# A two-layer graph network on one core: edge lists prepared in another order on three engines, and the first product in two float32r parts instead of plain float32

## The chip, the cores and the metric

The program runs on one core of a Trainium2 chip. The metric is the device time of one execution in microseconds; a kernel's time is the median of several executions. In the profile PE is TensorE, DVE is VectorE, ACT is ScalarE, POOL is GpSimd and SP is SyncE.

## The reference

There are 625 nodes with 512 features and 20,625 edges (10,000 drawn pairs in both directions, and a loop at each node).

```
layer 0:  xw = x @ W.T
          deg = counts of destinations (with a loop at each node), dinv = rsqrt(deg)
          h  = sum over edges of dinv[src]*dinv[dst]*xw[src], plus b
          h  = gelu(batch_norm(h)*gamma + beta) + x
          x1 = layernorm(x + h)
layer 1:  two RGCN layers with 2 relations: w[r] = sum over 30 bases of att[r,b]*basis[b]
          (30 x 512 x 512 for each layer), a gate sigmoid(x @ gate_w[r]) per edge,
          messages summed over edges, plus x @ root + bias; relu between them
          out = layernorm(x1 + that)
```

## The kernel before

The edges become two dense count matrices, one for each relation, held in `B` (sources by destinations, 5 chunks of 125 sources). `T` = 162 tiles of 128 edges in `NG` = 27 groups of six go through TensorE: for each group VectorE writes one-hot rows of the source's place in its chunk (`oh_src`) and of a key made of chunk, relation and the destination's place in a window of 16 nodes (`oh_key`), TensorE multiplies them into `psE` (two buffers), and VectorE adds two windows of each group to `B` (`add_window`). Edges are sorted by destination, so a window of 16 destinations holds three tiles; the first destination of each (`base`) is read into a register (`window_at`, one load for each window). Where a span of destinations is wider than a window, further rounds follow, under a branch on `more_i`; `rounds()` works that number out on VectorE.

All engines run programs written by hand, in order, with semaphores between them. What the change touches:

- **The front.** The three edge lists are loaded as integer rows (`edge_rows`), cast to float in one piece (`rows_f`), turned by TensorE (`edge`), copied out by VectorE, and the smallest and largest destination of each window go the same way (`mm`, `gmm`, `base`). A chain of small VectorE operations makes `place_pairs` and `key_pairs`.
- **The attention coefficients.** `att_t` is loaded on ScalarE's queue, spread by TensorE (`att`), and `build_S` makes from it the stationary operand `S` of the basis product. VectorE does this within group 0, ahead of the one-hots of group 1.
- **The basis product.** 64 loads of 1 MB go through a ring of four buffers (`basis_ring`, on SP's queue). Load n is issued when part n-4 has been used. `basis_part` multiplies a load on TensorE; four parts fill one half of `psW`; two halves are merged on ScalarE and VectorE (`w_first`, `w_merge`, `w_high`, `w_low`). The places of these parts in TensorE's order are written as numbers: `basis_upto(n)` does all parts up to n, and rounds down to whole pairs.
- **The first product.** `turn` transposes x and W in 128-blocks, `turned_out` copies them out on ScalarE, and `xw_part` does the 20 steps of x @ W.T in float32, between the groups of the loop.
- **After the loop.** VectorE sums the relations of `B` (`counts_of`, some by way of ScalarE) into `AT`; TensorE counts degrees (`deg`, 25 matmuls); POOL takes the power (`dinv_p`); ScalarE and VectorE make `z`, the scaled xw in two parts; `aggregate0(f, halves)` multiplies z by AT for the feature block f. Basis parts stand between these. After the blocks all parts up to 31 are done, and then the transposes `("g", c)` of the gelu's result. From there on nothing is changed but line numbers.

TensorE's main results go round four PSUM banks in the order of the list `uses`: a use waits until the one four places ahead of it has been released.

## Time and profile before

| | us |
|---|---|
| median of 3 runs (range) | 314.32 (312.93 to 317.32) |
| profiled execution | 314.59 |
| its span | 312.7 |
| TensorE matmuls busy | 276.0 (88%) |
| VectorE busy | 160.3 (51%) |
| ScalarE busy | 89.5 (29%) |
| mean granted clock | 0.96 |

The profiled execution is 0.3 us over the median, and 1.9 us of it lie outside the span. TensorE is the busiest engine as a mean, but a busy matmul in the profile includes its latency, and stages have limits of their own. The stages are: a front up to the first one-hot at 14.1 us; the 27 groups up to 78.4 us; degrees, z and the first aggregation up to 92.6 us; the other three feature blocks up to 118.7 us; and the rest.

### The profile page before, as it was taken

The page shows a single profiled execution, that of the slowest core. Times are in us where ns is not written, and L with a number is a line of the kernel's source. Part 1 is how long each engine was busy: PE and PEld are TensorE (multiplying, and loading weights), DVE is VectorE, ACT ScalarE, POOL GpSimd, SP SyncE. Part 2 cuts the span into 40 slices and gives each one's busy share as a digit, 9 for nine tenths or more (in the row PEclk, how much of TensorE's full clock was granted, in tenths as well). Part 3 has the DMA queues.
Part 4 walks back from the last instruction along what each step waited for, and adds up shares of the span by engine and source line. Part 5 has one row for each costly group of instructions (what it writes and reads, how often), then busy time and mean ns, then how long its engine had stood idle before and what let it go on. Part 6 is the DMA issues. An engine that isn't in the chain of part 4 may idle for free.

```text
span 312.7 us, 4598 instructions
## 1 busy us (share of the span) xinstructions
PE 276.0 (88%) x1687; PEld 180.8 (58%) x1687; DVE 160.3 (51%) x362; ACT 89.5 (29%) x140; POOL 38.3 (12%) x73
## 2 busy tenths in 40 slices
PE   1589958989799977679999999999997999999991
PEld 1573413433566643237765656677774878787770
DVE  3888888884656856855221241342434225334443
ACT  5160220201436876551352104112212242100000
POOL 2001000000292106500000000000005500011111
PEclk9999986999779999779999999999999999999997
DMA  6998992999989999958994897976002400001112
GB/s 164 231 418 326 353 410 80 415 375 369 364 259 307 413 398 426 371 183 299 388 379 171 366 343 283 419 286 265 21 1 52 118 0 0 0 2 33 33 33 66
DMA packets 12802, 73.63 MB, mean 235 GB/s; under 512 B 2000, under 2 KB 2243, under 8 KB 4588
## 3 DMA queue, kind: packets, MB, share of 16 engines
q1 hardware_dynamic: 11330, 70.82, 60.7%
q0 software_dynamic: 1104, 2.36, 2.9%
q8 instruction: 13, 0.21, 0.3%
q10 hardware_dynamic: 346, 0.17, 0.2%
q14 instruction: 9, 0.07, 0.1%
HBM read 72.05 MB, written 1.28 MB: 235 GB/s over the span
## 4 chain that ended last, share of the span: by engine, by line
PE 62%; DVE 16%; DMA 8%; issue 7%; DVEq 3%; ACT 1%; POOL 1%; ACTq 0%; POOLq 0%
PE psW L515 15%; PE psM L496 9%; PE psM L497 8%; PE psM L498 8%; PE psM L753 7%; DMA basis_ring<-in_L_gnn_basis_dram 7%; PE psM L773 6%; DVE B L1081 4%; DVEq L1071 2%; PE psM L563 2%; DVE oh_key L1088 2%; PE psE L596 2%; DVE oh_src L1088 2%; DMA rows_i<-in_edge_type_dram 1%; PE psM L639 1%
## 5 line engine op out<-in xcount | busy, mean ns | idle before, releaser
L515 PE MATMUL psW<-basis_ring,S 128*32 128x512 f32 x512 | 67.9, 646 | 6.3 <-DVEq L1057 3.7
L1267 DVE SCALAR_TENSOR_TENSOR zg<-psM,gate,zg 125x512 fp32r<-125x512 f32 x20 | 15.0, 751 | 56.9 <-ACT zg L929 56.9
L515 PEld LDWEIGHTS psW<-basis_ring,S 128*32 128x32 f32 x512 | 13.5, 114 | 41.2 <-issue 27.4
L496 PE MATMUL psM<-w,hlT 128*125 128x512 f32 x80 | 32.4, 405 | 0.1
L498 PE MATMUL psM<-w,hlT 128*125 128x512 f32 x80 | 31.7, 396 | 0.0
L497 PE MATMUL psM<-w,hlT 128*125 128x512 f32 x80 | 31.7, 396 | 0.0
L929 ACT ACTIVATE zg<-psM,gate 125x512 fp32r<-125x512 f32 x20 | 13.8, 688 | 46.3 <-PE psM L498 45.9
L596 PEld LDWEIGHTS psE<-oh_key,oh_src 128*125 128x125 f16 x162 | 13.9, 143 | 22.4 <-issue 17.3
L753 PEld LDWEIGHTS psM<-BB,zg 125*128 125x128 f32 x160 | 23.1, 188 | 3.4 <-issue 2.5
L753 PE MATMUL psM<-BB,zg 125*128 125x320 f32 (+1 forms) x160 | 24.1, 309 | 0.0
L773 PE MATMUL psM<-zg,BB 125*125 125x512 f32 x100 | 24.0, 394 | 0.0
L1081 DVE TENSOR_TENSOR B<-B,psE 125x160 f32 x54 | 17.5, 324 | 11.1 <-issue 6.6
L596 PE MATMUL psE<-oh_key,oh_src 128*125 128x160 f16 x162 | 17.0, 245 | 6.9 <-DVE B L1081 6.8
L563 PE MATMUL psM<-w0T,xT 128*125 128x512 f32 x40 | 21.7, 634 | 0.0
L773 PEld LDWEIGHTS psM<-zg,BB 125*125 125x125 f32 x100 | 18.6, 186 | 4.7
L480 POOL DMA_DIRECT2D root_raw<-in_L_gnn_root_dram x16 | 7.9, 501 | 106.8 <-DVE hlT L1297 106.8
L496 PEld LDWEIGHTS psM<-w,hlT 128*125 128x125 f32 x80 | 14.8, 185 | 9.0 <-issue 2.5
L1088 DVE TENSOR_TENSOR oh_key<-iota_f,key_pairs 128x960 f16<-128x960 f16 x27 | 17.7, 654 | 0.3
L498 PEld LDWEIGHTS psM<-w,hlT 128*125 128x125 f32 x80 | 14.8, 185 | 3.8
L497 PEld LDWEIGHTS psM<-w,hlT 128*125 128x125 f32 x80 | 14.8, 185 | 3.4
L1067 DVE TENSOR_TENSOR w<-w_both,w 128x512 fp32r<-128x512 f32 x16 | 13.1, 861 | 7.1 <-ACT w L816 6.5
L800 ACT ACTIVATE w_half<-psW,mask_h 128x512 f32<-128x512 f32 x16 | 10.1, 679 | 20.0 <-PE psW L515 20.0
(154 smaller groups left out, 381.0 us busy)
## 6 DMA issues: line engine op xcount, KB each, us to landing
basis_ring<-in_L_gnn_basis_dram SPq DMA_DIRECT2D x64, 1024.0 KB, 7.3
root_raw<-in_L_gnn_root_dram POOLq DMA_DIRECT2D x32, 64.0 KB, 3.6
xs<-in_x_dram SPq DMA_DIRECT2D x1, 1120.0 KB
out_dram<-xs SPq DMA_DIRECT2D x5, 224.0 KB
w_raw<-in_L_gnn_W_dram SPq DMA_DIRECT2D x4, 256.0 KB, 9.6
bias_b<-in_L_gnn_bias_dram POOLq DMA_DIRECT2D x1, 250.0 KB, 3.5
xs<-in_x_dram SPq DMA_DIRECT2D x1, 130.0 KB
out_dram<-xs SPq DMA_DIRECT2D x5, 26.0 KB
```

The lines of the kernel that those rows point to most:

```text
L496: nc.tensor.matmul(o, l_hi, r_hi, start=start, stop=False)
L497: nc.tensor.matmul(o, l_hi, r_lo, start=False, stop=False)
L498: last[0] = nc.tensor.matmul(o, l_lo, r_hi, start=False, stop=stop)
L515: m = nc.tensor.matmul(psW[32 * j:32 * j + 32, cc % 2, :], S[:, cc % 2, cc // CH, q].rearrange("p k r -> p (k r)"), ring[:, n % RING, j, : ...
L563: last[0] = nc.tensor.matmul(bank(("xw", c))[0:PC, :], xT[:, k, n], w0T[:, k], start=(k == 0), stop=(k == KC - 1))
L596: nc.tensor.matmul(psE[0:PC, g % 2, at:at + KEYS], oh_src[:, g % 3, j * P:j * P + PC], oh_key[:, t % OH, :], start=(j % SG == 0), stop=(j ...
L753: last[0] = nc.tensor.matmul(bank(("h", f, h))[:, 0:n], zg[:, i, d, r, f * P:(f + 1) * P], BB[:, at:at + n], start=(d + r + i == 0), stop= ...
L773: last[0] = nc.tensor.matmul(bank(("out", c))[0:PC, :], BB[:, at:at + PC], zg[:, i, d, r, :], start=False, stop=(d == NC - 1 and r + i == 2))
L929: nc.scalar.activation(zg[:, 0, c, r, :], bank(("Z", L, c, r))[0:PC, :], ACT.Copy, scale=gate[:, L, c, r:r + 1]).then_inc(zg_hi, 1)
L1081: v.tensor_tensor(to, to, psE[0:PC, g % 2, h * KEYS:(h + 1) * KEYS] .rearrange("p (c t w) -> p c t w", c=NC, t=R), ALU.add).then_inc(win_a ...
L1088: return v.tensor_tensor(out, pair.unsqueeze(1).broadcast_to(shape), pairs[:, first:first + n].unsqueeze(2).broadcast_to(shape), ALU.is_equal)
L1267: link(v.scalar_tensor_tensor(out=zg[:, 1, c, r, :], in0=bank(("Z", L, c, r))[0:PC, :], scalar=gate[:, L, c, r:r + 1], in1=zg[:, 0, c, r, ...
```

## The change

- The rows of destinations, sources and relations have semaphores of their own. VectorE casts only the destinations; ScalarE casts the other two, and copies the turned destinations out of PSUM. VectorE reads the turned sources and relations straight from PSUM. Chunk numbers come from a scaling and a rounding by a large constant, where four comparisons stood. Keys beyond a window are marked by 1024 in one combined operation.
- `B` is cleared by POOL, where ScalarE did it, and the number of further rounds is worked out by POOL, in the idle time of its front.
- `build_S` has four operations and no clearing, where it had eight and one.
- The register of `more_i` is loaded in group 14, and those of the last four windows in groups 23 to 26, between the two windows of the group, where all five stood behind the loop.
- x and W are held as an upper and a lower float32r part. TensorE turns them (`turn`), ScalarE copies the upper part out, TensorE multiplies it by the negative identity into the same bank (`take_upper`), and ScalarE copies the rest out. `xw_part` then does three float32r matmuls (`mm3`) for one in float32.
- All five chunks of x are turned before the loop, two of them and one `take_upper` ahead of the matmuls of att; W is turned in groups 2 and 3.
- In the loop the basis parts go up to 15 (17 before) and start at group 5 (3 before); parts 16 and 17 stand within the degrees, behind the second source chunk; 18 and 19 behind the transposes of vec; 20 and 21 behind the first aggregation. Block f = 1 is followed by 22 and 23 and block f = 2 by 24 to 27. The first merge moves from group 13 to 17, its lower part from 15 to 19.

```diff
-        for a in range(3):
-            use(("edge", a), "dve")
+        use("dst", "act")
         use("minmax", "dve")
+        use("src", "dve")
+        use("etype", "dve")
...
-        FIRST_IN = 23
+        FIRST_IN = 21
...
-        PARTS_IN = 17
-        FIRST_TURNS = 3
-        TURN_AT = {0: (3,), 1: (4, 5), 2: (6, 7), 3: (8,)}
-        ROUNDS_AT = 12
-        MERGE_AT = {13: 0}
-        LOW_AT = {15: 0}
+        TURN_AT = {0: (("rest", NC - 1),), 2: (("turn", NC), ("turn", NC + 1), ("rest", NC)),
+                   3: (("rest", NC + 1), ("turn", NC + 2), ("turn", NC + 3), ("rest", NC + 2)), 4: (("rest", NC + 3),)}
+        MERGE_AT = {17: 0}
+        MORE_AT = 14
+        LOW_AT = {19: 0}
...
+            def take_upper(i):
+
+                to, ps = turned_from(i)
+                if i == 0:
+                    pe.wait_ge(minus_ready, 1)
+                pe.wait_ge(in_half, i + 1)
+                nc.tensor.matmul(ps, minus[:], to[:, 0], start=False, stop=True, skip_group_check=True).then_inc(in_rest, 1)
+
             def xw_part(i):
 
                 c, k = i // KC, i % KC
-                n = slice(c * PC, (c + 1) * PC)
-                pe.wait_ge(in_turned, 3 + k if c == 0 else 1 + KC + c)
+                pe.wait_ge(in_turned, NC + 1 + k if c == 0 else NC + KC)
                 if k == 0:
                     wait_free(pe, ("xw", c))
-                last[0] = nc.tensor.matmul(bank(("xw", c))[0:PC, :], xT[:, k, n], w0T[:, k], start=(k == 0), stop=(k == KC - 1))
+                n = slice(k * PC, (k + 1) * PC)
+                mm3(bank(("xw", c))[0:PC, :], xT[:, 0, c, n], xT[:, 1, c, n], w0T[:, 0, k], w0T[:, 1, k], k == 0, k == KC - 1)
...
+            for i in range(AHEAD_OF_ATT):
+                turn(i)
+            take_upper(0)
             pe.wait_ge(att_in, 16 * 2)
...
-                for i in TURN_AT.get(g, ()):
-                    turn(i)
-                xw_upto(3 * (g - 2) // 4)
-                basis_upto(min(3 * g // 4 - 1, PARTS_IN))
+                for step, i in TURN_AT.get(g, ()):
+                    (turn if step == "turn" else take_upper)(i)
+                xw_upto(10 * (g - 4) // 11)
+                basis_upto(7 * g // 10 - 2)
...
             xw_upto(NC * KC)
-            basis_upto(19)
...
+                if s == AT_ORDER[1]:
+                    basis_upto(17)
             done()
...
-            basis_upto(21)
+            basis_upto(19)
...
+            for a, arrived in ((0, src_in), (2, etype_in)):
+                act.wait_ge(arrived, 16 * 2)
+                nc.scalar.activation(rows_f[:, a], rows_i[:, a], ACT.Copy).then_inc(side_rows, 1)
...
-            dve.wait_ge(edges_in, 16 * 6)
-            link(v.tensor_copy(rows_f[:], rows_i[:]))
+            dve.wait_ge(dst_in, 16 * 2)
+            link(v.tensor_copy(rows_f[:, 1], rows_i[:, 1]))
...
-                if g == ROUNDS_AT:
-                    rounds()
+                    if i == 0 and g == MORE_AT:
+                        dve.wait_ge(rounds_ready, 1)
+                        more = nc.values_load(more_i[0:1, 0:1], engines=[mybir.EngineType.DVE], min_val=0, max_val=N // W)
+                    if i == 0 and g >= NG - 4:
+                        late.append(window_at(NW - NG + g))
```

TensorE ahead of the first group (`psE`), before. `att_t` is the coefficients, `xs` is x, `w_raw` is W:

```order
L569 MATMUL psM<-gmm,ones_f 128x54
L575 MATMUL psM<-att_t,w_half 128x4 x4
L549 MATMUL psM<-ident,xs 128x125 x8
L552 MATMUL psM<-ident,w_raw 128x128 x4
L596 MATMUL psE<-oh_key,oh_src 125x160 x6
```

The same place after the change:

```order
L605 MATMUL psM<-gmm,ones_f 128x54
L575 MATMUL psM<-ident,xs 128x125 x8
L590 MATMUL psM<-xT,minus 128x500
L614 MATMUL psM<-att_t,w_half 128x4 x4
L575 MATMUL psM<-ident,xs 128x125 x4
L590 MATMUL psM<-xT,minus 128x500
L575 MATMUL psM<-ident,xs 128x125 x4
L590 MATMUL psM<-xT,minus 128x500
L575 MATMUL psM<-ident,xs 128x125 x4
L590 MATMUL psM<-xT,minus 128x500
L636 MATMUL psE<-oh_key,oh_src 125x160 x6
```

Between att and the first group stood three turns; now three turns and three subtractions stand there, each subtraction behind a copy of ScalarE.

VectorE at the end of the loop, before; an addition to `B` is a window, a load is of a register, and the last row and three more like it are followed by the last four windows:

```order
L1071 TENSOR_LOAD base_i
L1071 ISA x2
L1081 ISA
L1081 TENSOR_TENSOR B<-B,psE 125x10x16
L1081 ISA
L1081 TENSOR_TENSOR B<-B,psE 125x10x16
L1113 TENSOR_LOAD more_i
L1113 ISA x2
L1071 TENSOR_LOAD base_i
```

And after the change:

```order
L1125 TENSOR_LOAD base_i
L1125 ISA x2
L1135 ISA
L1135 TENSOR_TENSOR B<-B,psE 125x10x16
L1125 TENSOR_LOAD base_i
L1125 ISA x2
L1135 ISA
L1135 TENSOR_TENSOR B<-B,psE 125x10x16
L1135 ISA
L1135 TENSOR_TENSOR B<-B,psE 125x10x16
```

The run of five loads is gone: one load stands between the two windows of the last group, and the last four windows follow at once.

TensorE behind the loop, before (`psW` is two basis parts, `ones_r,AT` the degrees, `AT,z` the first aggregation):

```order
L563 MATMUL psM<-w0T,xT 125x512 x2
L515 MATMUL psW<-basis_ring,S 32x512 x8
L619 MATMUL psM<-ones_r,AT 125x2 x25
L626 MATMUL psM<-ident,vec_rows_q 128x8 x4
L515 MATMUL psW<-basis_ring,S 32x512 x8
L639 MATMUL psM<-AT,z 128x320 x2
```

And after the change:

```order
L659 MATMUL psM<-ones_r,AT 125x2 x10
L534 MATMUL psW<-basis_ring,S 32x512 x8
L659 MATMUL psM<-ones_r,AT 125x2 x15
L668 MATMUL psM<-ident,vec_rows_q 128x8 x4
L534 MATMUL psW<-basis_ring,S 32x512 x8
L682 MATMUL psM<-AT,z 128x320 x2
```

The pair that stood ahead of the degrees now stands within them.

## Rows read from the trace of the kernel before

**Rows 1.** The page: busy tenths, granted clock and DMA in 40 slices.

```profile
PE   1589958989799977679999999999997999999991
DVE  3888888884656856855221241342434225334443
PEclk9999986999779999779999999999999999999997
DMA  6998992999989999958994897976002400001112
```

**Rows 2.** Timeline of the front: start us, us, engine, line, operation, tiles, idle before.

```profile
6.14 0.56 DVE L973 CAST rows_f<-rows_i 81x768 f32<-81x768 int32 x1 [2.28 <-DMA rows_i<-in_edge_type_dram]
8.92 0.55 DVE L989 TENSOR_REDUCE gmm<-psM 1x54 f32<-1x162 f32 x2
...
12.36 1.86 PE L575 MATMUL psM<-att_t,w_half 30*128 30x4 f32 x8 [2.01 <-DMA att_t<-in_L_gnn_att_dram]
...
14.13 0.55 DVE L1088 TENSOR_TENSOR oh_src<-iota_f,place_pairs 128x756 f16<-128x756 f16 x1
...
14.15 1.93 PE L549 MATMUL psM<-ident,xs 125*128 125x125 f32 x8
...
15.27 1.12 DVE L1022 TENSOR_TENSOR S<-mask_k,psM 128x64 f32<-128x64 f32 x8
...
16.11 0.59 ACT L826 ACTIVATE xT<-psM 128x500 f32<-128x500 f32 x1 [0.24 <-PE psM L549]
...
16.90 0.55 DVE L1088 TENSOR_TENSOR oh_src<-iota_f,place_pairs 128x756 f16<-128x756 f16 x1
...
19.10 0.78 DVE L1081 TENSOR_TENSOR B<-B,psE 125x160 f32 x2
```

**Rows 3.** Timeline of the loop, groups 12, 13, 23 and 24.

```profile
37.62 0.55 DVE L1088 TENSOR_TENSOR oh_src<-iota_f,place_pairs 128x756 f16<-128x756 f16 x1
...
41.08 0.55 DVE L1088 TENSOR_TENSOR oh_src<-iota_f,place_pairs 128x756 f16<-128x756 f16 x1
...
48.08 1.03 PE L596 MATMUL psE<-oh_key,oh_src 128*125 128x160 f16 x6 [3.10 <-DVE B L1081]
...
65.63 0.55 DVE L1088 TENSOR_TENSOR oh_src<-iota_f,place_pairs 128x756 f16<-128x756 f16 x1
...
65.86 0.60 PE L596 MATMUL psE<-oh_key,oh_src 128*125 128x160 f16 x6 [0.48 <-DVE B L1081]
...
67.61 0.55 DVE L1088 TENSOR_TENSOR oh_src<-iota_f,place_pairs 128x756 f16<-128x756 f16 x1
```

**Rows 4.** The chain of waits, 72 to 92 us: start us, us, what.

```profile
73.64 0.01 DVEq L1113
...
75.82 0.30 DVEq L1071
...
76.60 0.33 DVE B L1081
...
78.04 0.34 DVE B L1081
...
80.40 3.17 PE psM L619 x25
...
85.72 3.64 PE psW L515 x16
```

**Rows 5.** The chain of waits, 92 to 120 us.

```profile
92.60 1.11 PE psM L661 x10
93.72 1.90 PE psW L515 x16
...
95.63 12.10 DMA basis_ring<-in_L_gnn_basis_dram
...
108.90 8.77 DMA basis_ring<-in_L_gnn_basis_dram
...
117.71 1.07 PE psW L515 x8
118.78 0.65 PE psM L677 x4
```

**Rows 6.** Windows of one microsecond: PE, PEld, DVE, ACT, POOL busy, PEclk, DMA share, GB/s.

```profile
79.00:80.00 1.00, 0.71 (x8) 0.00 (x0) 0.99 (x3) 0.47 (x1) 0.00 (x0) 1.00 1.01 426
...
81.00:82.00 1.00, 1.00 (x11) 1.00 (x10) 1.00 (x3) 0.72 (x1) 0.00 (x0) 1.00 1.13 287
...
83.00:84.00 1.00, 1.00 (x7) 0.97 (x7) 0.17 (x1) 0.00 (x0) 0.00 (x1) 0.50 0.95 344
...
89.00:90.00 1.00, 1.00 (x8) 0.71 (x5) 1.00 (x2) 0.00 (x0) 1.00 (x4) 0.68 0.69 225
```

**Rows 7.** Timeline of TensorE's and VectorE's operations that the new ones resemble.

```profile
20.46 1.02 PE L549 MATMUL psM<-ident,xs 125*128 125x125 f32 x8
...
28.40 1.06 PE L563 MATMUL psM<-w0T,xT 128*125 128x512 f32 x2
...
85.83 4.23 DVE L1169 SCALAR_TENSOR_TENSOR z<-xw,dinv_p,z 125x512 fp32r<-125x512 f32 x5 [0.32 <-POOL dinv_p L445]
...
250.02 0.39 PE L497 MATMUL psM<-w,hlT 128*125 128x512 f32 x1
250.25 0.40 PE L498 MATMUL psM<-w,hlT 128*125 128x512 f32 x1
```

**Rows 8.** The tile `basis_ring`: its DMAs from issue to landing.

```profile
DMA to landing us min/median/max: 4.6/7.3/18.5
```

More of the change, by code:

```diff
@@ L76 @@
 SWAPPED = [i ^ 1 for i in range(32)]
+FAR = 1024.0
+ROUNDING = 1.5 * 2.0 ** 23
 def gnn_block(nc, x, src, dst, etype, W0, b0, gamma, beta,
@@ L238, in use @@
             releaser.append(by)
-        for a in range(3):
-            use(("edge", a), "dve")
+        use("dst", "act")
         use("minmax", "dve")
+        use("src", "dve")
+        use("etype", "dve")
         use("base", "dve")
-        turned = [("xT", 0), ("xT", 1)] + [("w0T", k) for k in range(KC)] + [("xT", c) for c in range(2, NC)]
+        turned = [("xT", c) for c in range(NC)] + [("w0T", k) for k in range(KC)]
+        for name in turned[:AHEAD_OF_ATT]:
+            use(name, "act")
         use("att", "dve")
-        for name in turned:
+        for name in turned[AHEAD_OF_ATT:]:
             use(name, "act")
@@ L529, in _, with edges_turned @@
             pe.wait_ge(consts, 4)
[L530 to L532 removed]
+            def edges_turned(name, a):
+                wait_free(pe, name)
                 for h in range(2):
[L534 removed]
+                    last[0] = nc.tensor.transpose(bank(name)[:, h:T:2], rows_f[:, a, h, :],
                                                   ident[0:ROWS, 0:ROWS])
                 done()
+            pe.wait_ge(rows_ready, 1)
+            edges_turned("dst", 1)
             pe.wait_ge(minmax_ready, 1)
@@ L585, in xw_upto @@
                 steps_done[0] = max(steps_done[0], n)
-            for i in range(FIRST_TURNS):
+            for i in range(AHEAD_OF_ATT, NC):
                 turn(i)
+                take_upper(i - 1)
             for g in range(NG):
@@ L832, in xw_out @@
                 release(nc.scalar.activation(xw[:, c, :], bank(("xw", c))[0:PC, :], ACT.Copy), ("xw", c), "act")
-            for i in range(len(turned)):
-                turned_out(i)
+            turned_out(0, 0)
+            for i in range(1, NC):
+                turned_out(i, 0)
+                turned_out(i - 1, 1)
+            turned_out(NC - 1, 1)
+            for i in (NC, NC + 2):
+                turned_out(i, 0)
+                turned_out(i + 1, 0)
+                turned_out(i, 1)
+                turned_out(i + 1, 1)
             w_first(0)
@@ L1112, in _ @@
                     w_low(LOW_AT[g])
-            more = nc.values_load(more_i[0:1, 0:1], engines=[mybir.EngineType.DVE], min_val=0, max_val=N // W)
-            at = [window_at(w) for w in range(NW - 4, NW)]
             for i, w in enumerate(range(NW - 4, NW)):
-                add_window(w, at[i])
+                add_window(w, late[i])
             dve.wait_ge(win_added, NW)
             with dve.If(more > 0):
-                ROUND = 8
+                ROUND = 9
                 v.tensor_copy(tile_f[:].rearrange("p (g t) -> p g t", t=SG),
```

155 lines of the change are left out of this document (89 added, 66 removed).

## The prediction

> **What bounds the kernel now.** I read the page's slices first. TensorE shows nines almost everywhere from slice 18 on (counted from 0), but the eighteen before have gaps, the granted clock dips at slices 6, 10 and 11, and the DMA line is near nine for two thirds of the run [rows 1]. So I went through the stages by the timeline and the chain of waits, since the change touches only what lies before 118.78 us, where the transposes of the gelu's result start. What comes later keeps its order, and I let it move as one block.
>
> *The front* is a chain of small steps. VectorE casts the edges at 6.14, the ranges are found at 8.92, the first one-hot starts at 14.13. Beside it runs a second chain: the matmuls of att wait for their load until 12.36 and take 1.86 us, and VectorE builds S at 15.27, ahead of the one-hots of group 1 at 16.90. The first window goes in at 19.10 [rows 2].
>
> *The loop* is VectorE's. From one group to the next it takes 1.98 us (65.63 to 67.61), and TensorE waits for it (0.48 us ahead of its group) [rows 3]. Behind the last group VectorE stands from 73.64 to 76.60 with five register loads; the last window ends at 78.38 (78.04 + 0.34) [rows 4].
>
> *Degrees, z, first aggregation*: the 25 matmuls of deg run from 80.40 to 83.57, a basis pair from 85.72 takes 3.64 us at half clock, and the aggregation ends at 92.60 [rows 4, 5]. The clock reads 1.00 at 81 to 82, 0.50 at 83 to 84, and is on its way back at 89 to 90 (0.68) [rows 6].
>
> *The other blocks* end with the basis loads: the chain goes through a load from 95.63 for 12.10 us and another from 108.90 for 8.77 us, to the last pair's matmuls at 117.71 [rows 5].
>
> **The change, part by part**, as a sum of times against this execution.
>
> *Front.* The cast now waits for one list and has a third of the elements, the copies and eight operations of about 0.33 us go, and two wider ones come. By the spacing in the trace I put the first one-hot near 11 us where it was 14.13. But S is built from att, whose load is issued as before: it lands at 12.36, the matmuls end at 14.22 [rows 2]. So VectorE waits there; the 3 us shrink to the 1.05 us between 14.22 and 15.27. Building S took from 15.27 to 16.90, 1.63 us, for eight operations and a clearing; four operations of twice the width I take at 1.1, so 0.5 more is won. VectorE could add the first window at 19.10 - 1.5 = 17.6. TensorE must have done its first group by then. Behind att (14.22) stand three turns, three subtractions, and ScalarE's copies of 0.59 us between them [rows 2]. A turn costs 0.97 us as at 14.15 (1.93 for two) or 0.51 as at 20.46 (1.02 for two) [rows 2, 7]; the way is a turn, three copies and their handovers (0.1 each), a subtraction (0.23 to 0.46), and the group's 0.60: 14.22 + 0.5 to 0.97 + 2.1 + 0.3 + 0.6 gives 17.7 to 18.6 [rows 2, 3, 7]. I take 18.2: **-0.9**, between -1.5 and -0.4.
>
> *Loop.* The rounds went with 3.46 us for group 12 (37.62 to 41.08) where 1.98 is usual: -1.48 [rows 3]. Its cover on POOL is long: the number is first wanted at group 14, more than 20 us later. Five register loads come in between windows. One takes some 0.6 us (five in the 2.96 us) where nothing runs beside it [rows 4]; here it stands behind a window of 0.33 us, so I take 0.3 each, +1.5, between 0 and 3.0. The moved merge costs VectorE the same in both places. On TensorE a step of the product was 1.06 us, 0.90 of them to the next row, and is three matmuls of 0.23 us spacing now, 0.70 [rows 7]. With 0.60 for a group and a pair of basis parts of 1.90 us, at 10 steps in 11 groups and 7 parts in 10, that is 0.60 + 0.63 + 0.66 = 1.9 us for each group, below VectorE's 1.98 [rows 3, 5]. The product's saved 20 x 0.2 = 4 us are thus worth nothing by themselves: VectorE covers them. If VectorE were faster they would count. The nine subtractions (2.1 us) fall in the light groups 0 to 4. Loop: **0**, between -1.5 and +1.5.
>
> *Tail.* The five loads behind the loop are gone, and the last four windows must wait only for TensorE. But between its groups 25 and 26 stand a product step and a basis pair. Group 25 can start when group 23's windows are in, about 2.3 us ahead of where VectorE is done with group 24's; then 0.60 + 0.70 + 1.90 + 0.60 = 3.8 us to the end of group 26, 1.5 us past VectorE. Two windows and a handover end 0.9 later: 2.4 us in place of the 4.74 from 73.64 to 78.38 [rows 3, 4, 5, 7]. **-2.3**, between -3.0 and -1.5. The last window ends at 78.38 - 0.9 - 2.3 = 75.2.
>
> *Degrees.* The pair of basis parts ahead of the degrees was free: it filled a wait that ended at 80.40. Now a pair stands within them, and its full price lies on the path to dinv and z: +1.90 at full clock, +3.64 at half [rows 4, 5]. TensorE runs dry near 75.0 and gets the first sums near 77.2. Before, it ran dry at 79.7 and the clock fell near 83, 3.2 us later [rows 6]; the same distance now gives 78, just where the new pair starts (77.2 + 10 of 25 matmuls, 1.3). I take the middle, **+2.8**. The degrees end at 83.57 - 3.2 + 2.8 = 83.2.
>
> The Trainium skill has half rate as TensorE's resting state, lifted by sustained work and taken back after idling ("TensorE: Matmul & The Clock Gate", the part on the clock gate). Taken strictly, the pair would be slow throughout, and the sum would end 0.9 us later than mine; the row at 81 to 82, still at 1.00 a good microsecond after the gap, speaks for part of it being fast.
>
> *z and the first aggregation.* VectorE's last z ends at 90.06, 6.5 us behind the degrees [rows 7]. The old pair waited for the merge and blocked TensorE until 89.36; the new one (parts 18, 19) has its halves ready, runs right behind vec and is done 2.5 to 4.3 us behind the degrees. The aggregation then follows z, and ends 7.2 us behind the degrees at the earliest, 9.0 (as before) at the latest. I take 7.4: **-1.6**. It ends at 83.2 + 7.4 = 90.6, 2.0 us earlier than 92.60.
>
> *Blocks 1 to 3.* Every pair is one later, and behind block 2 stand two pairs. The ring has four buffers, so loads 28 to 31 are issued only as 24 to 27 are used, behind block 2. The last of four follows its use by the least latency of 4.6 us and three more loads; a load comes each 2.5 us when the queue is full (10 us for the four from 107.7 to 117.7) [rows 5, 8]. Loads 24 to 27 wait less than now, but four parts on TensorE where two stood are 1.9 us. From block 2's start at the old distance, the last load's matmuls end about 1.5 us later than now: **+1.5**, between 0 and +2.5.
>
> Sum: -0.9 + 0 - 2.3 + 2.8 - 1.6 + 1.5 = -0.5. With 1.9 us outside the span the profiled execution of 314.59 becomes 314.1; by the median of 314.32 it is 313.8. I forecast **314.0**, no change that can be told: what the front and the tail give, att's load and the later basis parts take. This case's own range, by its bounds, is 311.0 to 317.5.
>
> **The rivals.**
>
> *The gain is kept* (faster). This needs the later loads to cost nothing and the clock to hold. For it: the queue has room, since DMA reads 2 in slice 6 and 5 in slice 17 [rows 1]. Against it: the chain's 12.10 and 8.77 us [rows 5]. Price: front -1.5, loop -1.5, tail -3.0, degrees +1.9, z -1.8, blocks 0: -5.9, 308.5. Should a later clock dip vanish as well, 307.
>
> *TensorE becomes the loop's bound at half clock* (slower). The place is behind the merge in group 17. A group at half clock takes 1.03 us for 0.60 [rows 3]; product and pair scale to 1.27 and 1.27 (0.35 of 3.64), 3.6 us against 1.98. TensorE may lag by some 2.5 us before VectorE waits, so from the second slow group on each costs 1.6. Before, the clock came back within 6 us at no visible cost, as the dip's row shows VectorE ahead of TensorE by 3.10 [rows 3]. With five such groups 5.5 us are added: 319.5.
>
> *ScalarE's copies hold the first group* (not what it says). If turns stay at 0.97 and each handover costs 0.3, the first window comes at 20 rather than 18.2, and the two heavy groups 2 and 3 pass their delay on: +2.5, 316.5.
>
> **How the numbers follow.** Chances: forecast 0.52, gain kept 0.24, loop at half clock 0.11, held by ScalarE 0.13. The predicted time is the forecast's, 314.0. The range runs from 308.3 to 318.8: it takes in half the gain-kept case or more, and part of the slow loop. Two per cent (6.3 us), about what a measurement can tell from no change, is below 308.0 and above 320.6. Faster gets 0.14 (half of the gain kept, a little for surprises), slower 0.07, the same 0.79.
>
> **What would show it.** Right: VectorE idle ahead of S, ended by TensorE's att near 14.2; the first window near 18.2; groups still 1.98 apart; the last window near 75; deg broken by a basis pair and ending near 83; the aggregation at 90 to 91; a DMA of `basis_ring` last in the chain near 117 to 118. Wrong: a first one-hot followed at once by S, TensorE's groups starting late in the loop, windows in groups 23 to 26 as fast as the others, or a last load that lands several microseconds earlier. The prediction fails above all if the basis loads are not what ends the blocks, since then the 2 us won ahead of them, or more, come through.

## The result and the profile after

The changed kernel takes **320.0 us** (median of 19 runs, 317.7 to 321.9); the kernel before takes 314.7 beside it (19 runs). The ratio is 1.0156, with a 95% interval of 1.013 to 1.018. It is 1.6% slower (4.9 us by the ratio), clear of the noise, where I had forecast no change at 314.0 within 308.3 to 318.8. An execution more than 1.5% above the fastest of its kernel counts as slow and enters no ratio below; the profiled executions of b_parts_late (324.5 us) and p_earlier (319.0 us) are of that kind.

The profiled execution of the changed kernel took 319.76 us, span 317.8, against 314.59 and 312.7. Where do these 5.1 us of span lie? I cut both traces at the same events:

| stage, by what ends it | before | after | difference | predicted |
|---|---|---|---|---|
| front: first window starts | 19.10 | 19.41 | +0.3 | -0.9 |
| loop: group 24's windows end | 73.64 | 74.99 | +1.0 | 0 |
| tail: last window ends | 78.38 | 77.54 | -2.2 | -2.3 |
| degrees: copy of deg starts | 83.59 | 85.66 | +2.9 | +2.8 |
| z and first aggregation end | 92.60 | 94.61 | -0.1 | -1.6 |
| blocks: gelu's transposes start | 118.78 | 124.55 | +3.8 | +1.5 |
| all that follows | 312.7 | 317.8 | -0.7 | 0 |

The page's slices of the changed kernel (busy tenths, the granted clock, DMA; compare [rows 1]): DMA has a 3 in slice 3 and a 4 in slice 7, counted from 0.

```profile
PE   1897996986989985769999999999997999999991
DVE  6668878876355842983420141252325125334443
PEclk9999999799769998968999999999999999999998
DMA  6993799488799999986994979977201400001112
```

The timeline of its front (start us, us, engine, line, tiles, idle before):

```profile
2.40 2.75 POOL L442 MEMSET B<- 125x3200 f32 x1
...
2.45 2.79 DVE L1029 CAST ident<-ident 128x128 bf16<-128x128 f32 x1 [2.32 <-POOL BB L439]
2.59 2.71 DVE L1030 CAST ones_r<-ones_f 125x128 fp32r<-125x128 f32 x1
...
6.29 0.27 DVE L1041 CAST rows_f<-rows_i 81x256 f32<-81x256 int32 x1
...
10.54 1.93 PE L575 MATMUL psM<-ident,xs 125*128 125x125 f32 x8 [0.87 <-DMA xs<-in_x_dram]
...
12.40 0.76 PE L590 MATMUL psM<-xT,minus 128*128 128x500 f32 x1
...
13.09 1.87 PE L614 MATMUL psM<-att_t,w_half 30*128 30x4 f32 x8
...
14.99 0.88 DVE L1085 TENSOR_TENSOR S<-mask_k,psM 128x128 f32<-128x128 f32 x4 [1.27 <-PE psM L614]
...
18.69 0.58 PE L636 MATMUL psE<-oh_key,oh_src 128*125 128x160 f16 x6
...
19.41 0.78 DVE L1135 TENSOR_TENSOR B<-B,psE 125x160 f32 x2 [1.14 <-PE psE L636]
```

The cast of the destinations starts at 6.29, no earlier than the 6.14 of [rows 2]: VectorE's two first casts lie under GpSimd's clearing of `B`. Att's matmuls come 0.7 us later than in [rows 2], now behind the turn of x and a subtraction that waits for ScalarE's copy. So S is built at 14.99 where I had 14.22. Then three more turns and subtractions run until 18.7, and the windows stand waiting for TensorE (1.14 us).

The chain of waits of the changed kernel, 72 to 125 us (start us, us, what; compare [rows 4] and [rows 5]):

```profile
76.06 0.57 PE psE L636 x6
...
77.21 0.34 DVE B L1135
...
79.19 1.39 PE psM L659 x10
80.58 3.32 PE psW L534 x16
83.90 1.74 PE psM L659 x15
...
89.64 4.97 PE psM L682 x20
...
102.69 1.90 PE psW L534 x16
104.61 7.91 DMA basis_ring<-in_L_gnn_basis_dram
...
112.56 1.11 PE psW L534 x8
...
113.68 9.76 DMA basis_ring<-in_L_gnn_basis_dram
...
123.48 1.06 PE psW L534 x8
```

The basis pair stands within the degrees and takes 3.32 us, at a granted clock of 0.57 between 80 and 84 us (the windows below), close to the lower of the two levels (1.2 GHz). The chain then goes through two loads, as it did before, but the last one lands at 123.44, not at 117.67.

What the load queue did in between is seen in the windows by stage. Columns: stretch, its length, busy time of PE, PEld, DVE, ACT, POOL, the granted clock, DMA share, GB/s. First the kernel before:

```profile
24.00:28.00 4.00, 3.70 (x29) 1.54 (x18) 3.40 (x9) 0.00 (x0) 1.26 (x1) 1.00 0.84 295
28.00:42.00 14.00, 13.72 (x100) 5.70 (x100) 11.57 (x31) 1.86 (x3) 0.00 (x0) 1.00 0.94 359
42.00:56.00 14.00, 9.42 (x54) 3.88 (x58) 12.23 (x27) 2.50 (x3) 0.00 (x0) 0.76 0.58 231
56.00:70.00 14.00, 13.16 (x99) 5.75 (x92) 11.72 (x28) 1.86 (x3) 0.00 (x0) 1.00 0.99 399
...
24.00:90.00 66.00, 57.67 (x383) 25.22 (x372) 52.44 (x118) 12.97 (x20) 7.18 (x11) 0.90 0.85 328
...
90.00:124.00 34.00, 30.74 (x255) 20.13 (x253) 20.07 (x59) 22.11 (x32) 12.28 (x19) 1.00 1.02 377
```

and the changed kernel:

```profile
24.00:28.00 4.00, 2.95 (x27) 1.81 (x29) 3.56 (x8) 2.56 (x5) 1.04 (x1) 1.00 0.09 35
28.00:42.00 14.00, 12.76 (x103) 6.78 (x96) 11.94 (x29) 1.86 (x3) 0.00 (x0) 1.00 0.79 304
42.00:56.00 14.00, 10.38 (x81) 5.38 (x79) 11.24 (x27) 2.77 (x3) 0.00 (x0) 1.00 1.00 386
56.00:70.00 14.00, 12.51 (x85) 7.39 (x86) 11.64 (x26) 2.35 (x4) 0.00 (x0) 0.88 0.61 225
...
80.00:84.00 4.00, 4.00 (x22) 1.26 (x21) 1.17 (x2) 0.55 (x1) 0.00 (x0) 0.57 0.62 209
...
24.00:90.00 66.00, 54.70 (x395) 29.30 (x394) 50.47 (x112) 15.46 (x25) 4.88 (x6) 0.93 0.77 290
...
90.00:124.00 34.00, 29.24 (x236) 20.12 (x235) 17.89 (x54) 20.06 (x31) 9.81 (x20) 0.94 1.01 374
```

From 90 us on the queue is full in both kernels. Between 24 and 90 us it moved 290 GB/s in the changed kernel and 328 before: 38 GB/s over 66 us are 2.5 MB, and at 374 GB/s that is an estimate of 6.7 us. The last load is 5.8 us later. That is the theory the experiments had to test: **the later places of the basis parts leave the load queue idle in the loop, and nothing gives the time back, since the queue is full from 90 us on.**

### The profile page after: what moved, and what is told of

It is laid out like the page before. It is cut to its first block, busy times and chain, and to the rows that moved or that the text cites. A ratio compares the mean times of both kernels' runs of the same rounds, so it can differ in the third digit from the quotient of the medians.

```text
span 317.8 us, 4664 instructions
## 1 busy us (share of the span) xinstructions
PE 279.4 (88%) x1716; PEld 191.8 (60%) x1716; DVE 159.5 (50%) x345; ACT 92.9 (29%) x152; POOL 44.2 (14%) x85
## 4 chain that ended last, share of the span: by engine, by line
PE 66%; DVE 14%; DMA 8%; issue 6%; DVEq 2%; ACT 1%; POOL 0%; SPq 0%; POOLq 0%; ACTq 0%
PE psW L534 13%; PE psM L515 10%; PE psM L517 9%; PE psM L516 9%; PE psM L796 7%; PE psM L816 6%; DMA basis_ring<-in_L_gnn_basis_dram 6%; DVE B L1135 4%; DMA xs<-in_x_dram 3%; PE psE L636 3%; PE psM L682 3%; DVE x_sum L1278 1%; PE psM L575 1%; DVEq L1125 1%; DVE oh_key L1142 1%
## 5 line engine op out<-in xcount | busy, mean ns | idle before, releaser
L534 PE MATMUL psW<-basis_ring,S 128*32 128x512 f32 x512 | 64.6, 622 | 4.5 <-DMA basis_ring<-in_L_gnn_basis_dram 4.4
L859 ACT ACTIVATE w<-w_both 128x512 fp32r<-128x512 f32 x16 | 13.0, 847 | 11.3 <-DVE w_both L1102 10.6
L682 PEld LDWEIGHTS psM<-AT,z 125*128 125x128 f32 x80 | 13.5, 217 | 4.4 <-issue 4.4
```

Of the source, the lines that this page charges most:

```text
L534: m = nc.tensor.matmul(psW[32 * j:32 * j + 32, cc % 2, :], S[:, cc % 2, cc // CH, q].rearrange("p k r -> p (k r)"), ring[:, n % RING, j, : ...
L682: last[0] = nc.tensor.matmul(bank(("agg0", f, h))[:, 0:n], z[:, i, s, f * P:(f + 1) * P], AT[:, s, a:a + n], start=(s == 0 and i == 0), st ...
```

## The experiments

Ratios are to the kernel before, run on the same chip beside each. "Profiled" is the time of the profiled execution; the column GB/s is the rate of all DMA between 24 and 90 us in it, and "landed" is when the last load in the chain ahead of the gelu's transposes landed in it.

The kernel before read 314.7 beside the changed kernel and 313.9 to 314.2 beside the others, so the difference of two medians is not quite the difference of two kernels. Where I write "by the ratios", it is the difference of two ratios, times 314 us, with the two intervals put together.

| kernel | median us | ratio [95%] | profiled us | GB/s | landed |
|---|---|---|---|---|---|
| the changed kernel | 320.0 | 1.016 [1.013, 1.018] | 319.8 | 290 | 123.44 |
| a_double_early | 318.9 | 1.015 [1.011, 1.019] | 318.2 | 290 | 122.98 |
| a_clear_act | 318.7 | 1.015 [1.011, 1.019] | 319.1 | 296 | 123.91 |
| a_loop_back | 317.4 | 1.011 [1.007, 1.016] | 317.2 | 306 | 121.83 |
| a_pair_ahead | 316.0 | 1.006 [1.004, 1.009] | 318.3 | 308 | 121.73 |
| p_earlier | 315.9 | 1.005 [1.002, 1.008] | 319.0 | 322 | 120.85 |
| p_loads_behind | 314.5 | 1.001 [0.998, 1.004] | 314.7 | 323 | 117.76 |
| the kernel before | 314.7 | 1 | 314.6 | 328 | 117.67 |
| c_within | 313.8 | 0.999 [0.996, 1.001] | 312.3 | 325 | 116.92 |
| p_fourth | 312.8 | 0.995 [0.991, 0.998] | 313.3 | 332 | 116.34 |
| a_parts_back | 312.6 | 0.995 [0.990, 1.000] | 313.1 | 331 | 116.06 |
| p_turns | 311.8 | 0.992 [0.989, 0.995] | 311.9 | 338 | 115.04 |
| p_front | 311.0 | 0.992 [0.989, 0.995] | 310.9 | 336 | 115.58 |

The time follows the landing of that load: from it to the end of the profiled execution it is 195.2 to 197.0 us in every row but p_earlier's, 198.2. The landing follows the rate before 90 us only roughly; p_earlier with 322 GB/s lands 3 us later than p_loads_behind with 323.

**a_parts_back**: the changed kernel with the basis parts at their places of before, all else as changed.

```diff
-        FIRST_IN = 21
+        FIRST_IN = 23
-                basis_upto(7 * g // 10 - 2)
+                basis_upto(min(3 * g // 4 - 1, 17))
+            basis_upto(19)
             wait_free(pe, "deg")
-                if s == AT_ORDER[1]:
-                    basis_upto(17)
-            basis_upto(19)
+            basis_upto(21)
```

> The changed kernel with the basis parts alone put back where the kernel before had them (17 in the loop, starting at group 3, 18 and 19 ahead of the degrees, 20 and 21 behind vec, 22 and 23 behind the first aggregation); front, product and merges stay as changed. Theory LOADS: in the changed kernel the load queue stands idle between 56 and 70 us because the ring is full (225 GB/s where it was 399), and from 90 us on it is full to the end of the blocks; two parts later are 2 MB later, some 5 us. Then this kernel gets 4 to 6 us back, 314 to 316, and the last load of the blocks lands near 118. Theory PATH: the time is lost on the way to z (half clock on the pair within the degrees, late first window), and the loads only follow. Then the pair out of the degrees gives 1.9 to 3.3 us back in the end of the first aggregation, and the whole gains no more than that: 317 to 318. Theory LOOP: two more parts in the loop make TensorE its bound (0.60 + 0.63 + 0.70 us for a group against 1.98), and little is gained: 319 to 320.

Measured 312.6. By the ratios the places alone are worth 6.5 us (4.8 to 8.2), about the whole slowdown or more; the rest of the change is 1.6 us faster than the kernel before (by the interval 0.1 to 3.1). Its chain of waits:

```profile
79.51 3.53 PE psM L660 x25
...
85.19 3.47 PE psW L534 x16
88.66 3.09 PE psM L681 x20
...
107.75 8.31 DMA basis_ring<-in_L_gnn_basis_dram
116.11 1.07 PE psW L534 x8
```

The degrees start 0.3 us later than in the changed kernel and still the last load lands 7.4 us sooner. Three things of the places are undone at once here; the single ones come below.

**b_parts_late**: the converse, the kernel before with the changed places (and its merges at the changed groups, `MERGE_AT = {17: 0}`, `LOW_AT = {19: 0}`).

> The kernel before with the changed kernel's places of the basis parts and of the first merge alone (15 in the loop, 16 and 17 within the degrees, 18 and 19 behind vec, 20 and 21 behind the first aggregation, four behind block 2; merge in group 17, its lower part in 19). Theory LOADS: the mirror of the other run, 4 to 6 us slower than before, 319 to 321, with the last load of the blocks landing 5 us later. Theory PATH: slower by the pair within the degrees alone, 1.9 to 3.6 us, 316.5 to 318. If the places don't matter: 314.5.

Measured 322.3, ratio 1.023 [1.017, 1.030]: 7.3 us above the kernel before (5.3 to 9.3), somewhat more than I expected. So the price belongs to the places, not to their meeting with the new product or front. (Its profiled execution took 324.5 us, well above its median, so it has no row in the table.)

**a_half_loads**: the changed kernel with loads 20 to 35 cut to half their bytes. This leaves half of those basis matrices' data out of the computation.

```diff
+                w = 2 * D if 20 <= n < 36 else 4 * D
-                sp.dma_start(ring[:, n % RING].rearrange("p j o -> p (j o)"), rows[c // 2, c % 2]) \
+                sp.dma_start(ring[:, n % RING].rearrange("p j o -> p (j o)")[:, 0:w], rows[c // 2, c % 2][:, 0:w]) \
```

> The changed kernel with half of the bytes left out of the basis loads 20 to 35 (the other half of each buffer keeps what an earlier load put there, so the output is not the reference's). TensorE's work, order and all waits stay. Theory LOADS: blocks 1 to 3 stop being bound by loads; the matmuls of parts 28 to 31 follow block 3, the transposes of the gelu's result start near 118 where they started at 124.5, and the total falls by 5 to 7 us, to 313 to 315. Theory PATH: waits on loads are only where the time shows; the total falls by less than 2 us.

Measured 316.0, ratio 1.007 [1.002, 1.013], less gained than I expected. The chain no longer has a load in it:

```profile
108.93 3.57 PE psW L535 x32
...
117.45 1.59 ACT w L860 x2
...
121.38 0.72 PE psM L721 x4
```

With these bytes gone the transposes start 3.2 us sooner (121.38, not 124.55); by the ratios the kernel gains 2.6 us (0.7 to 4.5), by the medians 4.0. So the changed kernel does wait for bytes here. Behind them the four parts at once on TensorE and the merges on ScalarE come up as the next limit. What share of the slowdown is bandwidth this run can't say, since the kernel before waits for loads too and wasn't run with half of them.

**a_clear_act**: the changed kernel with `B` cleared by ScalarE, as before, in place of GpSimd's memset.

```diff
-            nc.gpsimd.memset(counts, 0.0).then_inc(b_clear, 1)
-            act.wait_ge(b_clear, 1)
+            link(nc.scalar.activation(counts, ones_f[0:PC, 0:1].broadcast_to(list(counts.shape)), ACT.Copy, scale=0.0))
```

> The changed kernel with B cleared by ScalarE, behind its copy of the destinations and the negative identity, where POOL did it. In the changed kernel POOL's memset runs from 2.40 to 5.15 us and VectorE's two casts that start at 2.45 and 2.59 end only at 5.24 and 5.30 (0.23 and 0.22 us before). Theory PORT: the memset holds the casts up; without it they take 0.2 us again, VectorE is done with its constants near 3.9, casts the destinations when they land (about 5.2 in place of 6.29) and starts the first one-hot some 1 us earlier, near 11.5. What follows is held by att (15.0) and by TensorE's turns, so the total gains 0 to 0.5 us: 319.5 to 320. If the casts stay at 2.7 us, something else held them. If the front's time comes through to the end: 319.

Measured 318.7, not told apart from the changed kernel by its interval. Its timeline shows the casts at their old length:

```profile
2.45 0.23 DVE L1028 CAST ident<-ident 128x128 bf16<-128x128 f32 x1 [2.31 <-POOL BB L439]
2.59 0.22 DVE L1029 CAST ones_r<-ones_f 125x128 fp32r<-125x128 f32 x1
...
10.69 0.55 DVE L1141 TENSOR_TENSOR oh_src<-iota_f,place_pairs 128x756 f16<-128x756 f16 x1
...
15.65 0.88 DVE L1084 TENSOR_TENSOR S<-mask_k,psM 128x128 f32<-128x128 f32 x4 [3.75 <-PE psM L612]
```

The first one-hot comes 1.8 us earlier, and VectorE waits 3.75 us for att instead of 1.27. So the clearing did hold the casts, and the gain is lost in the wait for TensorE's matmuls of att.

**a_pair_ahead**: the changed kernel with parts 16 and 17 ahead of the degrees (`basis_upto(17)` in front of `wait_free(pe, "deg")`) instead of within them.

> The changed kernel with basis parts 16 and 17 moved from within the degrees to ahead of them; the loop keeps 15, the other places stay as changed. Theory PAIR: the pair within the degrees lies on the path to z (79.19 to 85.64 us for the degrees with it, 3.5 without) and pays 1.9 at full and 3.6 at half clock, while TensorE idles 1.85 us ahead of the degrees; ahead of them half of it is hidden. The degrees end 1.5 to 3 us earlier, and as every later load is bound to a part's use, the whole gains the same: 317 to 318.5. Theory LOADS alone: what counts is how many parts are used by the end of the loop; this pair is used some 2.6 us earlier, but the following ones keep their places, so the gain is 1 us at most: 319 to 320. In either case it stays well above the 312.6 us of the kernel whose parts are all put back; what is left over is the one pair in the loop, which doubles the parts behind block 2.

Measured 316.0, below both of my ranges: a gain of 2.9 us by the ratios (1.7 to 4.1); by the medians it is 4.0. In the profiled executions the last load lands only 1.7 us sooner (121.73). But this one is the longest of its eight, 318.3 us where the median is 316.0, and so only 1.5 us below the changed kernel's: the trace shows a worse execution than the median, and the two don't contradict each other.

**p_fourth**: a_parts_back with a fourth matmul, lower by lower part, in each of the 20 steps of the product.

```diff
+                last[0] = nc.tensor.matmul(bank(("xw", c))[0:PC, :], xT[:, 1, c, n], w0T[:, 1, k], start=False, stop=(k == KC - 1))
```

> The kernel with its parts put back, and a fourth float32r matmul (lower part by lower part) in each of the 20 steps of the first product, so that a step takes 0.93 us of TensorE, as much as the float32 step before the change (0.90 to the next row). Theory COVER: VectorE sets the pace of the loop and the product's saving is worth nothing, so 4.6 us more of TensorE's work cost nothing: 312 to 313.5. Theory WORK: TensorE is so close to the pace that the whole of it comes out at the end: 316 to 317. Between: TensorE reaches 2.16 us in groups 5 to 24 and holds VectorE up by 0.1 to 0.2 us each: 314 to 315.

Measured 312.8 against 312.6, ratio 0.995 in both: 20 more matmuls cost nothing that can be told (by the ratios within 1.8 us). VectorE covers the product, so what the change saved on it was worth nothing either, as the prediction had it.

**p_loads_behind**: a_parts_back with the last four windows' register loads behind the loop again.

```diff
-                    if i == 0 and g >= NG - 4:
-                        late.append(window_at(NW - NG + g))
+            late = [window_at(w) for w in range(NW - 4, NW)]
```

> The kernel with its parts put back, and the registers of the last four windows loaded behind the loop again, as before the change (that of the further rounds stays in group 14). In the changed kernel the two windows of groups 23 to 26 stand 0.75 us apart where they stood 0.46, so a load costs 0.3 us there, 1.2 for four; behind the loop four loads take 4 x 0.62 = 2.5 us less what TensorE is behind (0.2 to 0.8 us of waiting that VectorE has there now). Expected: 1 us slower, 313.5 to 314. Rival: with its parts put back TensorE's last group is not behind, the loads are nearly free in either place: 312.6.

Measured 314.5, so the moved loads win 1.9 us by the ratios, only just clear of the noise (0.2 to 3.6). The degrees start at 79.50 against 79.51 in the profiled executions; what differs there is that they take 4.94 us instead of 3.53, and the last load lands 1.7 us later. TensorE had idled 1.79 us ahead of the degrees here and 0.29 in a_parts_back, and its granted clock reads 0.50 from 80 to 81 us here, 1.00 there. By these two executions the gain of the move comes less from an earlier end than from the shorter gap, with the clock up for longer behind it; that the gap is the cause is not shown by two traces.

**p_front**: a_parts_back with `B` cleared by ScalarE, att's matmuls ahead of the first `take_upper`, and the turns of x's chunks 2 to 4 moved behind groups 0 and 1.

```diff
-        TURN_AT = {0: (("rest", NC - 1),), 2: ...
+        TURN_AT = {0: (("turn", 2), ("rest", 1), ("turn", 3), ("rest", 2)), 1: (("turn", 4), ("rest", 3), ("rest", 4)), 2: ...
-            take_upper(0)
             pe.wait_ge(att_in, 16 * 2)
...
-            for i in range(AHEAD_OF_ATT, NC):
-                turn(i)
-                take_upper(i - 1)
+            take_upper(0)
             for g in range(NG):
```

> The kernel with its parts put back, B cleared by ScalarE, the matmuls of att ahead of the first subtraction, and the turns of x's chunks 2 to 4 with their subtractions moved from ahead of the first group into groups 0 and 1. Now the first window waits 1.14 us for TensorE's first group, which waits for ScalarE's copies. Theory HELD: without that the first window comes 1 to 2 us earlier, near 18.3, the loop keeps its pace, and as loads are used earlier too the whole gains it: 311 to 311.6. Rival: the turns in groups 0 and 1 delay the groups behind them, and group 4 or 5 has lost it again: 312.6. Rival: the loads bound blocks 1 to 3 whatever the front does: 312.6, with the gain visible up to the first aggregation.

Measured 311.0, the best kernel of the study: by its ratio 0.8% [0.5, 1.1] faster than the kernel before, which the change set out from. The first window starts at 17.79; with the changed kernel's order it starts at 19.41, and at 19.3 to 20.4 in the experiments that keep that order. So TensorE's order ahead of the loop had held it. Against a_parts_back the gain in time is 1.6 us by the medians and 1.0 by the ratios, and not clear of the noise (within 1.8 us).

**p_turns**: the same without the clearing by ScalarE.

> The kernel with the old places, with att's matmuls ahead of the first subtraction and three turns moved behind groups 0 and 1, but B cleared by GpSimd as in the change. Together with ScalarE's clearing this gave 310.98 (312.62 without either). If the order of TensorE's work sets the front (ORDER), the clearing by GpSimd costs nothing here, since VectorE waits for att's matmuls anyway (3.36 us in that kernel): 311.0 +- 0.5, the first window near 18.0. If the casts that GpSimd's clearing stretches from 0.23 to 2.8 us are still in the way (CLEARING), the first one-hot stays at 12.5, the first window comes near 19, and the time is 311.8 to 312.6.

Measured 311.8, ratio 0.992 as p_front's, and the first window starts at 17.39. The earlier window is thus owed to the order of TensorE's work and not to the clearing, of whose worth in time nothing can be told.

**c_within**: a_parts_back with parts 18 and 19 within the degrees, behind their first ten matmuls.

> The kernel with the basis parts at their old places (312.62 measured), and one thing of the change put back: the last pair ahead of the degrees (parts 18 and 19) stands within them, behind the first ten of the 25 matmuls. Taking the pair out of the degrees won 320.0 - 316.0 = 4.0 us in the other direction. If the place within the degrees has a price of its own (ADD), this kernel ends 3 to 4 us above 312.6: 315.6 to 316.6, with the degrees' copy 2 to 3.5 us after 83.06. If the price was only paid because every pair was late already (TOGETHER: one late pair is absorbed while the load queue is full behind it), it is 312.6 to 314.0, with the degrees' copy late all the same and the last load's matmuls where they were, near 116 us.

Measured 313.8: by the ratios 1.2 us above a_parts_back and not told apart from it (within 1.7 us), as in the second of my two readings. The copy of deg is late by 0.7 (83.79), and the pair ran at full clock:

```profile
80.17 1.85 PE psW L534 x16
82.02 1.74 PE psM L661 x15
```

A pair at this place takes 3.32 us in the changed kernel and 1.85 here. That the price of a place depends on the other places is thus likely, but the times don't show it: 2.9 us (1.7 to 4.1) there and 1.2 us (-0.5 to 2.9) here overlap.

**p_earlier**: p_front with parts 16 and 17 behind group 21 (was 23), 18 and 19 behind group 25.

```diff
-                basis_upto(min(3 * g // 4 - 1, 17))
+                basis_upto(3 * g // 4 - 1 if g < 21 else 17 if g < 25 else 19)
```

> The kernel of 310.98 with three pairs of basis parts earlier still: parts 16 and 17 behind group 21 (was 23), 18 and 19 behind group 25 in the loop (was behind the loop). If the loads' start sets the end of the blocks (LOADS), the queue's idle stretch at 56 to 70 us (277 of some 400 GB/s) is used earlier and the last load's matmuls come 0.5 to 2 us sooner than 115.6: 309.0 to 310.5. If TensorE has no room left in the last groups (ROOM), the windows of groups 23 to 26 slip by a pair's 1.9 us, the degrees are later, and the time is 311.5 to 313.

Measured 315.9, by the ratios 4.3 us slower than p_front (3.0 to 5.6): neither of my two ranges. Its chain shows why:

```profile
60.22 1.90 PE psW L532 x16
...
62.13 7.67 DMA basis_ring<-in_L_gnn_basis_dram
...
69.84 1.69 PE psW L532 x8
```

and its timeline, what that meant for TensorE and VectorE:

```profile
69.84 1.69 PE L532 MATMUL psW<-basis_ring,S 128*32 128x512 f32 x8 [2.26 <-DMA basis_ring<-in_L_gnn_basis_dram]
...
72.66 0.32 DVE L1130 TENSOR_TENSOR B<-B,psE 125x160 f32 x1 [3.63 <-PE psE L631]
```

The load was asked for when part 13 had been used, at 62.1, and landed 7.67 us later; TensorE, in order, stood 2.26 us for it in the middle of the loop, the one-hot groups stood behind it, and VectorE waited 3.63 us. The degrees then start at 82.47, not at 78.47 as in p_front. This execution is 3.1 us above its kernel's median, but up to 64.8 us its trace agrees with p_front's within 0.1 us, and the wait follows there. A pair that is wanted sooner than its load can make the round of the ring holds everything. So the places have a bound on either side.

**a_double_early** and **a_loop_back** take the last two of the places singly, in the changed kernel: `FIRST_IN = 23`, by which the second pair moves from behind block 2 to behind the first aggregation; and the loop's rule `basis_upto(min(3 * g // 4 - 1, 17))`, which leaves all places behind the loop as changed.

> The changed kernel (320.0), with one place other: the second of the two pairs that it has behind block 2 is moved up, so that two pairs stand behind the first aggregation and one behind each of blocks 1 to 3. Two readings of the runs so far. BYTES: the basis loads fill the queue from 90 us on in every kernel, and what they miss between 24 and 90 us (the queue moved 290 GB/s there in the changed kernel, 331 with the old places: 2.7 MB in 66 us, 6 to 7 us at 360 to 420 GB/s) can't be had back. Then this move, all behind 90 us, gives little: 318.5 to 320, the last load landing at 122 to 123.5 us as before. PAIRS: four parts on TensorE where two stood, and four loads issued only then, are what costs; then it gives most of the 3.4 us that lie between 316.0 and 312.6: 316.5 to 317.5.

> The changed kernel (320.0), with the rule for the basis parts in the loop alone put back to that of before (17 parts' worth in the loop, each pair one to three groups earlier), and all places behind the loop as changed. So no pair stands within or ahead of the degrees, and two stand behind block 2. BYTES: the queue's gaps at 28 to 42 and 56 to 70 us close, the rate between 24 and 90 us rises from 290 to 310 to 320 GB/s, and the last load lands 3.5 to 5.5 us sooner than at 123.4; the degrees too are free of a pair: 314.5 to 316.5. PAIRS (the double pair behind block 2 and the places around the degrees are what costs, not the loop's rule): 317 to 318.5.

a_double_early measured 318.9, and its ratio is the changed kernel's: the double pair behind block 2 costs nothing that can be told (0.2 us by the ratios, within 1.6). a_loop_back measured 317.4, 2.6 us less by the medians and 1.4 by the ratios, not clear of the noise (within 1.7); the last load lands 1.6 us sooner, where I had expected 3.5 to 5.5. Its windows say why:

```profile
80.00:84.00 4.00, 4.00 (x23) 3.74 (x27) 1.24 (x3) 0.22 (x2) 0.43 (x1) 0.50 0.02 4
84.00:90.00 6.00, 5.78 (x34) 3.08 (x27) 5.28 (x8) 3.28 (x5) 5.91 (x10) 0.79 0.55 182
```

With the loop's places back and no pair at the degrees, the ring is full at 80 and the queue stands: 4 GB/s. What was won in the loop was lost there. By its number this run fell to the second reading, yet a_double_early rules out the double pair: what is left of that reading is the pair missing at the degrees, and it costs by the idle queue. In a_loop_back, a_pair_ahead and p_earlier, as in the changed kernel, the parts up to 19 are all that TensorE has used when 90 us come, so at most 24 loads can have been asked for (a load n is asked for when part n-4 has been used); in all the kernels at 314.7 and below the pair of parts 20 and 21 is done between 87.3 and 90.2, which asks for two loads more. In the others it starts only at 91.6 to 96.0, or ends at 92.4 (p_earlier). Where it is done in time, the kernel takes 311 to 314.7, else 316 to 320. This is read off one trace for each kernel; no run moved that one pair alone.

## Why the prediction was wrong

**The step that failed is "Blocks 1 to 3"**: +1.5 (0 to +2.5), measured +3.8, with the last load landing at 123.44 where I had forecast 117 to 118. It took the way from block 2's start to the last load as a distance, lengthened by two more parts on TensorE, and let the load move with the block. But the chain's two loads were in its own rows [rows 5], and a full queue behind 90 us has a date of its own: one pair fewer used at 90 us is two loads later at the end, 5 us by the 2.5 us a load that I had myself read off. The prediction used this number to place the four loads against one another and not against the queue's past. The queue's room in the loop I looked at only in the rival of the kept gain, and there as a reason why later loads might cost nothing; room that isn't used while it is there is the cost. a_parts_back and b_parts_late show that the places are the price, a_half_loads that bytes are waited for; a_double_early shows that the double pair, on which my +1.5 rested, was not the price.

The same step also made the sum itself the wrong form. If a load's date ends the blocks, what is won ahead of them doesn't come through unless it also brings parts forward. The prediction's last sentence had the opposite case only. So the table's split of the miss of about 5.6 us (2.3 in the blocks, 1.5 in z, 1.2 in the front, 1.0 in the loop, a little back elsewhere) isn't a split by causes.

**z and the first aggregation** (-1.6, measured -0.1): the pair behind vec was ready, as said, but TensorE was still at half clock, and the 20 matmuls took 4.97 us. a_parts_back shows 3.09 for them.

**Loop** (0, within -1.5 to +1.5, measured +1.0): the mechanism held. The two windows added in each of groups 23 to 26 start 0.76 apart (73.91 and 74.67) against 0.46 in the groups without a load, 0.3 for each register load as estimated; the rounds' stretch was gone. The rest was lost early: the one-hots of group 3 start 0.3 us later than before, those of group 7 1.2 us later (28.89 against 27.73). I had let the subtractions fall in the light groups 0 to 4 at no price; what delays groups 3 to 6 no run separates. One of these one-hots, at 26.52, takes 1.20 us instead of 0.55 and starts during a copy by GpSimd (26.26 to 27.30); whether that copy held it wasn't tested.

**Front** (-0.9, measured +0.3): VectorE did wait for att, as said. I had att's matmuls at 12.36, where they were, though the `order` rows had them behind x's turn and a subtraction; I didn't charge the copy by ScalarE between those two. (The sum for the first group, as written, ends at 18.2 and not at 18.6.) It is the rival "ScalarE's copies hold the first group" in part: 19.4 lies between its 20 and my 18.2. p_front and p_turns show that another order brings the first window to 17.4 to 17.8.

The rival in which the gain is kept needed later loads to cost nothing; they cost 6.5 us.

**The range** was too narrow by its own terms: the bounds of the six, added straight to the median of 314.3, run from 308.4 to 320.0 and not from 311.0 to 317.5. Front and blocks came out beyond their bounds, the other four within.

**Right**: the tail (-2.2 for -2.3) and the worth of the product (p_fourth). The degrees came out at +2.9 for +2.8, in part by luck: I took the middle between a fast and a slow pair, and the pair was slow nearly throughout (3.32 us, where 3.64 is the price at half clock), while the 25 matmuls around it took 3.13 us, as before (3.17). The rival of a loop bound by TensorE didn't come: at half clock (0.57 in 56 to 60 us) groups and products ran on with VectorE ahead for some us, as before. The Trainium skill has half rate come back after idling ("TensorE: Matmul & The Clock Gate", Part 1, on the clock gate). Taken as strictly as in the prediction, this fits the pair of the changed kernel, 3.32 us, and not c_within's pair at the same place, 1.85.

What stays open: why two pairs within the degrees behind like gaps (1.85 and 2.14 us) met different clocks, and whether the pair of parts 20 and 21 alone, moved ahead of 90 us, would give the whole loss back.

## What to carry to other kernels

When a stretch ends by loads through a full queue, ask how many buffers had been used when the queue became full, not how far the consumer is from the end; a consumer that is moved back by one place in an idle stretch is paid as whole loads at the end. Count the uses by that time in both kernels, and check the other side too: a use ahead of its load's round through the ring blocks all that the engine has behind it. And of a long sum of stages, find the one date that no stage moves before adding.

## What the chip showed beside this

A memset of 125x3200 by GpSimd (2.75 us) held two casts of VectorE that take 0.23 and 0.22 us alone: they took 2.79 and 2.71 and ended with it, at 5.2 us. In a_clear_act, without the memset, they took 0.23 and 0.22. The Trainium skill ("SBUF — State Buffer", "SBUF: two separate sides") has it that the two engines share a pair of ports which one instruction holds to its end; the rows agree. It was hidden here by the wait for att.

The clock after a gap isn't a fixed price: a pair of parts within the degrees took 3.1 to 3.3 us where TensorE had been idle for 1.83 to 1.85 us ahead of them (the changed kernel, a_clear_act, a_double_early), and 1.85 us behind an idle 2.14 us (c_within). Each of these is one execution.
